# One more product a batch on the identity in the third layer's attention

## The reference, cut to what matters

```python
xn = layernorm(x, ln_x_g, ln_x_b)              # context, 77 rows
ln = layernorm(latents, ln_l_g, ln_l_b)        # the batch's tokens, 128 rows
q = ln @ Wq.T
kv = jnp.concatenate([xn @ Wkv.T, ln @ Wlkv.T], axis=1)
...
attn = jnp.einsum('bhid,bhjd->bhij', qn, kn)
attn = jnp.where(full_mask[:, None, None, :], attn, -jnp.finfo(attn.dtype).max)
attn = jax.nn.softmax(attn, axis=-1)
out = jnp.einsum('bhij,bhjd->bhid', attn, v)
...
return out @ Wo.T + bo
```

## Time and profile before

| what | us |
|---|---|
| median of 3 runs (2425.81 to 2431.57) | 2430.26 |
| the profiled execution | 2425.89 |
| its span, first to last instruction | 2424.1 |
| PE busy over the span | 1992.0 (82%) |
| DVE busy | 1543.0 (64%) |
| ACT busy | 1111.8 (46%) |
| POOL busy | 990.0 (41%) |
| this stage, first scores to last projection | 1331.1 to 1515.5 |

### The profile page before, as it was taken

How to read it: one execution, slowest core, us unless ns; L and a number is a source line. 1 busy time by engine, 2 the same in 40 slices (tenths; PEclk the granted TensorE clock), 3 DMA queues, 4 the chain that set the end, 5 groups by cost and what they waited for, 6 DMA issues and landing times. The chain is left out here.

```text
span 2424.1 us, 39136 instructions
## 1 busy us (share of the span) xinstructions
PE 1992.0 (82%) x14355; PEld 1416.5 (58%) x14355; DVE 1543.0 (64%) x3706; ACT 1111.8 (46%) x2201; POOL 990.0 (41%) x886
## 2 busy tenths in 40 slices
PE   5887799789999976854593889799589888879998
PEld 3666599667777754431592556466367566554443
DVE  6996522358787755969214784511598689966775
ACT  4886444234444432325331665433144476644443
POOL 3454165344443214647566641171575200112332
PEclk9997799799999988975796796899699999999999
DMA  3000478321112126989891100343231100012221
GB/s 112 1 2 2 143 240 243 105 70 58 57 54 78 37 67 179 327 257 312 265 314 47 25 10 1 124 116 90 66 120 50 41 2 2 2 37 74 79 79 48
DMA packets 138277, 238.45 MB, mean 98 GB/s; under 512 B 20755, under 2 KB 66748, under 8 KB 133970
## 3 DMA queue, kind: packets, MB, share of 16 engines
q1 hardware_dynamic: 114216, 173.65, 21.7%
q0 software_dynamic: 23872, 62.29, 9.1%
HBM read 161.89 MB, written 73.99 MB: 97 GB/s over the span
## 5 line engine op out<-in xcount | busy, mean ns | idle before, releaser
L432 POOL TENSOR_TENSOR L1x_soft<-L1x_soft,L1x_rinv 128x616 f32<-128x616 f32 x64 | 77.6, 1214 | 190.7 <-DVE L1x_rinv L355 190.6
L2147 ACT ACTIVATE L3f_hT<-banks,L3f_b 128x512 f32<-128x512 f32 x128 | 88.0, 687 | 137.3 <-PE banks L2166 130.5
L2092 DVE TENSOR_TENSOR L3f_hT<-L3f_hT,L3f_spread 128x512 f32<-128x512 f32 x128 | 99.8, 803 | 35.1 <-ACT L3f_hT L2147 32.7
L2179 PE MATMUL banks<-L3f_hT,L3f_w 128*128 128x512 f32 x256 | 121.4, 598 | 0.0
L2166 PE MATMUL banks<-L3f_xT,L3f_w 128*128 128x512 f32 x256 | 120.1, 593 | 0.6 <-PEq L730 0.6
L2657 POOL DMA_INDIRECT L0e_rows<-xn_rows,L0f_token_of x78 | 77.9, 999 | 98.8 <-issue 63.5
L887 POOL TENSOR_TENSOR L0x_soft<-L0x_soft,L0x_rinv 128x1232 f32<-128x1232 f32 x32 | 71.9, 2247 | 101.1 <-DVE L0x_rinv L812 101.1
L2976 ACT ACTIVATE L0e_hT<-banks,L0e_w 128x256 f32<-128x256 f32 x156 | 69.2, 473 | 91.8 <-PE banks L3019 91.8
L2657 POOL DMA_INDIRECT L1h_rows<-xn_rows,L1f_token_of x72 | 74.9, 1041 | 76.4 <-POOLq L2410 46.7
L404 ACT COPY L1x_attnT<-banks 128x512 f32<-128x512 f32 x64 | 37.5, 585 | 148.0 <-PE banks L513 147.9
L266 DVE COPY L1x_keys<-banks 128x308 f32<-128x308 f32 x112 | 52.0, 464 | 68.8 <-PE banks L461 68.7
(11 more groups left out here) (598 smaller groups left out, 5876.8 us busy)
## 6 DMA issues: line engine op xcount, KB each, us to landing
hidden<-L1h_hid SPq DMA_DIRECT2D x24, 768.0 KB, 5.5
L0e_w<-in_L0f_w SPq DMA_DIRECT2D x39, 320.0 KB, 4.6
L0e_w<-in_L0f_w SPq DMA_DIRECT2D x39, 258.0 KB, 3.7
L1x_flat_values<-L1x_staged SPq DMA_DIRECT2D x34, 256.0 KB, 2.0
L1x_vals<-L1x_flat_values SPq DMA_DIRECT2D x14, 616.0 KB
mixed<-L1m_out SPq DMA_DIRECT2D x32, 256.0 KB, 4.1
L3f_spread<-L3f_gates SPq DMA_DIRECT2D x8, 1024.0 KB, 7.3
L3x_keys<-L_keys SPq DMA_DIRECT2D x5, 1232.0 KB
```

The lines of the kernel that those rows point to most:

```text
L432: pool.tensor_tensor(tile, tile, rinv[n % 2][:, :].unsqueeze(2).to_broadcast([P, U, NK]), ALU.mult).then_inc(probs_ready, 1)
L2092: dve.tensor_tensor(tile, tile, spread[t % 2][:, e, :], ALU.mult).then_inc(weighed, 1)
L2147: act.activation(hT[m % 3][:, c, :], hid_bank[(FC * m + c) % 4][:, :], ACT.Relu, bias=b1[:, FC * e + c:FC * e + c + 1]).then_inc(hid_out, 1)
L2179: last = pe.matmul(bank[:, :], w2[:, e, c, :], hT[m % 3][:, c, :], start=False, stop=(e == E - 1 and c == FC - 1))
```

## The change

A new function issues one product: the identity as weights, the identity three times over as the moving operand (128x384), into columns 128 to 511 of `out_bank`, which nothing reads. It waits for nothing and signals nothing. It is called once a step for n = 0 to 31, behind `scores(n+1)` and ahead of the jobs of place 2; in step 31, which has no scores, it follows `project(28)`.

```diff
@@ -1748,6 +1748,10 @@
             pe.matmul(proj_bank[:, 0:P], attnT[n % 2][:, :], latent.wo[:, :], start=True, stop=True).then_inc(proj_done, 1)
 
+        def keep_warm(pe):
+
+            pe.matmul(out_bank[:, P:4 * P], ident[:, :], ident[:, :].unsqueeze(1).to_broadcast([P, 3, P]), start=True, stop=True)
+
         block = ctx.enter_context(nc.Block())
         AHEAD = 17
 
@@ -1837,6 +1841,8 @@
                     project(pe, n - 3)
                 if 0 <= n + 1 < NBATCH:
                     scores(pe, n + 1)
+                if 0 <= n < NBATCH:
+                    keep_warm(pe)
                 for job in jobs_at(n, 2):
                     do_job(pe, job)
```

## The result

The change takes 2418.86 us (median of 8 runs, 2409.99 to 2422.55) against 2429.48 us for the kernel before in the same series (8 runs, 2424.94 to 2431.57): a ratio of 0.9962, 95% interval 0.9948 to 0.9977, or 10.6 us. 2424 was forecast, with a range of 2411 to 2437. In a second series it was 2420.99 against 2423.12: 0.9993, 0.9979 to 1.0006, which by itself can't be told from no change. The kernel before took 2429.48 in the first series, but 2424.42, 2423.92, 2423.12 and 2425.36 in the four others, so most of the difference between the two gains lies on its side. The whole program gained somewhere between 2 and 11 us, and against those four medians 2 to 6.5 (across series, so only as a guide). What follows is told from the stage, where the change repeats.

The account below looks back on a forecast made before the run. PE was taken to be on the path in most of the stage's 78.3 us at half clock. Terms -11 - 6.5 + 9.8 + 1.5 = -6.2 us took 2425.9 to 2419.7, with 4.4 for a median 2424; range 2411 to 2437.

Parts of the forecast that it names:

- The price of a product: Each of 32 added PE products takes 0.65 us at full clock, 1.58 at half; all on the path at full clock, 20.8.
- What hides it: PE's waits cover part of the products; at full clock 0.7 us a turn remains before batch 20, 2.1 from there, 9.8 together.
- What the clock gives back: Of 23.8 us available if all half-clock stretches of the stage go, 11 come at the end and 6.5 before 1476.
- the last stretch at half clock: The 37.5 us at the end of the stage with PE at half clock, to go nearly whole, giving 11 us.
- the 57% taken: Before 1476 in the stage, 6.5 of the 11.4 us available from the clock were expected to come.
- the part said to lose 2.3 us: The stage without its end: forecast to get 2.3 us slower, while the end gains 8.5.
- The sum: Over the stage, -11 - 6.5 + 9.8 + 1.5 = -6.2 us, which comes through to the kernel's time.
- the forecast's case: Half clock in the stage partly lifted, kernel at 2424 us, own range 2416 to 2431; chance 0.48.
- Rival B: All half clock behind batch 3 goes and 8 us of products are paid: -16 us, 2414; chance 0.20.
- C: Rival: half clock not lifted, products cost PE time at the stage's end and in half-clock stretches: +17 us, 2447; chance 0.15.
- D: Rival: last half-clock stretch only shortened by half (-6), 3 us gained before 1476: +3 us, 2433; chance 0.17.
- The rule against it: Transposes don't engage PE's full clock; if the new instruction counted as one, nothing is given back and C's sum holds.

Follow-up runs that it names:

- the second profile of before: The kernel before, unchanged, run and profiled again: 2425.84 us against 2425.36 us for the kernel before in its series, ratio 1.0010.
- the kernel with steps 23 to 31: The change with its product issued only in steps 23 to 31 instead of 0 to 31: 2420.99 us against 2424.42 us for the kernel before, ratio 0.9984.

## Why the prediction was right

*The price of a product* was forecast at 0.65 us; from start to next start it is 0.75 to 0.85 in the profile after, and on the path 0.66 in a first batch and 0.84 in a third.

*What hides it.* Up to batch 19 the products of a first and second batch were to vanish in the wait for DVE. They did: 9.17 us for batches 12 and 13 in both kernels. PE's wait there fell from 11.1 to 6.5 us, near the 6 forecast. The third batch was forecast at 0.5 and pays 0.84, and the fourth stays at 7.03 where it was 6.97, instead of the 0.2 forecast: 0.9 a turn instead of 0.7. From batch 20 on: 0.66 + 0.06 + 0.84, and a fourth batch pays 0.65 (7.03 against 6.38 in the second profile of before, the first window below). That is 2.2, and 2.1 was forecast. The next turn, batches 24 to 27, pays less, 1.4: the second window is again that profile, the fence behind it the kernel with steps 23 to 31. This step held.

```profile
1461.67:1468.05 6.38, 5.24 (x33) 3.40 (x33) 4.49 (x18) 4.64 (x12) 2.75 (x2) 1.00 0.00 0
1468.06:1484.81 16.75, 13.47 (x107) 9.85 (x107) 10.97 (x36) 12.41 (x44) 5.66 (x3) 0.99 0.01 1
1475.10:1479.04 3.94, 3.51 (x32) 2.83 (x31) 1.53 (x4) 3.34 (x14) 0.00 (x0) 1.00 0.01 2
```

```profile
1465.52:1483.71 18.19, 16.50 (x115) 11.12 (x115) 11.08 (x36) 12.56 (x44) 5.67 (x3) 1.00 0.00 1
```

*What the clock gives back.* Forecast was 17.5 us less 1.5 for products at half clock; with up to 5 x 0.9 + 2.2 + 1.4 + 2.2 = 10.3 us paid, the stage's 9.3 mean up to some 20. One rate was too low: for the third batch at the end the prediction took 4.47 us as full clock, a row at 0.87; at full clock it is 3.94 (the last window of the first fence above), so half clock cost it 2.34 us and not 1.81. The two halves were off: the last stretch at half clock went whole as forecast, but before it half clock fell from 41 to 14 us, more than the 57% taken. So the part said to lose 2.3 us gained 2.1 or 6.2, and the end gained 7.2 or 2.7, not 8.5. The reason given, that some falls would stay since no product lies in the 1.85 us wait, is too weak: one 3.4 us stretch is left between 1340.5 and 1460.

*The sum* was -6.2 us for the stage, -9.3 is measured. The first series' -10.6 lies between the forecast's case and B. That the kernel's time lies near the forecast is in part luck: the errors of the two halves of the stage offset each other in part, and in the second series the kernel gained 2.1 us. Rival B was nearer in the half clock left (17 of 78), but its 16 us would have needed products at 8 us and all of the clock. C is refuted for this product by its clock, and the product of 1 row shows what it would have been. D is out: where the last stretch stood the clock is 1.00.

*The rule against it* didn't bite. The new instruction stands as two passes (64 matmuls), so the change alone says nothing on it. But six one-pass transposes of 4-byte floats hold the clock as well, 0.94 and 0.96: here the trace disagrees with the Trainium skill ("TensorE: Matmul & The Clock Gate", section "Part 4: PE-mode transpose"), and the measurement decides.

*What stays open* is why the kernel gained 10.6 us in one series and 2.1 in another with the same stage. Of the 8.5 us between them, 6.4 are the kernel before (2429.48 and 2423.12) and 2.1 the change. In the profiles of all these kernels the stage begins between 1325.2 and 1335.1 us and what follows it takes 908 to 918 us, in code that none of them changes, with clock falls at other places. That is as large as the gain. Whether the changed stage also makes the next ones worse on average wasn't separated from that.

## What to carry to other kernels

Where PE is on the path at half clock though it is nearly always busy, look at how many rows its products use: filler of 1 row and of 64 rows made this kernel slower, of 128 rows faster. Then put the filler ahead of the instruction that waits rather than behind it: there the same products cost nothing in first and third batches up to batch 23 (behind it, 0.84 us a turn before batch 20 and 1.5 in the turn from batch 20 on). Judge by the stage in two profiles of either kernel, and compare times only within a series: elsewhere the clock moves a program of this kind by as much as such a change is worth.

## What the runs showed of the hardware

A contraction over 1 row takes PE as long as one over 128 (0.78 and 0.75 us for 384 columns in two passes, at full clock and ahead of the same instruction), but it doesn't act on the clock in the same way: half clock in the stage was 99 us with 1 row, 69 with 64, 17 with 128, and 78 without the product. The 1-row product also loads weights of 1 row, so these runs don't tell whether the rows of the weights or those of the moving operand count. The values don't have to be dense: the operand that held the clock is the identity, nearly all zeros (no run tried other values). Six 128x128 transposes of 4-byte floats take 0.71 us and do the same as the product, 21 us of half clock.

The same instructions can run with the clock falling elsewhere: the kernel before had 3.4 us of half clock in batches 14 and 15 in one profile and 13.7 in the other, while the change had its 17 us in the same batches both times.
